# Convolution stage: token records in groups of 128, a fixed index table for the scatters, and a store of the sums of its own

## What is computed

```
x = x + conv3x3(quantize(layernorm(x)), quantized w)      # "the sums", called x3
t = tokens(x)                                             # 50176 tokens of 128 channels
h = layernorm(t) @ W_gat                                  # 16 features of a token
a_src, a_dst = (h * att_src).sum(-1), (h * att_dst).sum(-1)   # 4 heads each
# per edge: e = leaky_relu(a_src[src] + a_dst[dst]); softmax over the edges of dst; weighted sum of h[src]
```

## Time and profile before

| | us |
|---|---|
| median of 3 runs | 10784.39 |
| the runs | 10778.33 to 10784.59 |
| the profiled execution, its time | 10787.32 |
| its span, first to last instruction | 10785.5 |
| first scatter of `convolve` starts | 4175.63 |
| last scatter of `convolve` ends | 4801.45 |

### The profile page before, as it was taken

One profiled execution on the slowest core, in us unless ns is written; L12 is line 12 of the kernel. 1 busy time (PEld: TensorE's weight loads), 2 busy tenths in 40 slices (PEclk: granted clock), 3 DMA queues, 4 the chain that ended last, 5 costly groups with the idle time before them and its releaser, 6 DMA issues. The chain is left out here.

```text
span 10785.5 us, 111540 instructions
## 1 busy us (share of the span) xinstructions
PE 4563.0 (42%) x31813; PEld 2715.7 (25%) x31813; DVE 5474.9 (51%) x14162; ACT 3929.5 (36%) x9657; POOL 6184.6 (57%) x6259
## 2 busy tenths in 40 slices
PE   0011777777758997873222222223223223223000
PEld 0011555555544444541111111111111101101000
DVE  9987999999986775541121121121121112112487
ACT  0011888888854554332121111112112112112255
POOL 0000555555532224667777777777777777777675
PEclk9755999999978998876666666666666666666555
DMA  0000111111121223543222222222222222222366
GB/s 20 2 0 34 40 39 38 39 41 38 39 78 55 62 62 100 141 121 55 44 46 49 44 46 49 44 42 53 44 42 53 44 42 53 44 42 48 134 250 244
DMA packets 1326096, 663.81 MB, mean 62 GB/s; under 512 B 1058255, under 2 KB 1239100, under 8 KB 1320764
## 3 DMA queue, kind: packets, MB, share of 16 engines
q1 hardware_dynamic: 1142396, 576.49, 19.5%
q0 software_dynamic: 183104, 80.22, 5.7%
HBM read 344.86 MB, written 313.71 MB: 61 GB/s over the span
## 5 line engine op out<-in xcount | busy, mean ns | idle before, releaser
L1832 POOL DMA_INDIRECT gr_rec<-rec,gr_idx x4096 | 3954.2, 965 | 1248.8 <-issue 1248.0
L1853 PE MATMUL gr_p_h<-gr_tT,gr_w 128*128 128x512 f32 x1568 | 849.4, 696 | 3671.7 <-ACT gr_hT L1887 3638.7
L1972 DVE TENSOR_SCALAR gr_pen<-gr_same 128x64 f32<-128x64 f32 x64 | 13.7, 213 | 3170.6 <-DMA gr_rec<-rec,gr_idx 3170.6
L1853 PEld LDWEIGHTS gr_p_h<-gr_tT,gr_w 128*128 128x128 f32 x1568 | 347.6, 227 | 4154.9 <-ACT gr_hT L1887 3723.8
L544 POOL TENSOR_TENSOR at_sq<-at_qk 128x256 f32<-128x256 f32 x392 | 290.2, 740 | 1844.1 <-ACT at_qk L594 1843.9
L1900 ACT ACTIVATE gr_ee<-gr_dd 128x512 f32<-128x512 f32 x64 | 40.3, 629 | 3588.0 <-DVE gr_dd L1991 3588.0
L1858 PE MATMUL gr_p_y<-gr_hT,gr_w 128*128 128x512 f32 x1568 | 688.9, 592 | 0.0
L1952 DVE STREAM_TRANSPOSE gr_z<-gr_yb 128x2048 f32<-128x2048 f32 x98 | 226.5, 2311 | 902.8 <-issue 491.5
L1887 ACT ACTIVATE gr_hT<-gr_p_h,gr_b 128x512 f32<-128x512 f32 x784 | 517.6, 688 | 191.7 <-PE gr_p_h L1853 191.0
L2140 POOL DMA_INDIRECT cb_a<-scan,cb_idx x392 | 499.0, 1273 | 133.7 <-issue 122.4
L1340 POOL DMA_INDIRECT adst<-co_rec,co_idx x448 | 424.5, 948 | 223.3 <-issue 123.1
(11 more groups left out here) (358 smaller groups left out, 13212.1 us busy)
## 6 DMA issues: line engine op xcount, KB each, us to landing
y<-gr_z SPq DMA_DIRECT2D x392, 256.0 KB, 5.4
cb_y<-y SPq DMA_DIRECT2D x28, 3584.0 KB, 13.2
gr_rec<-rec,gr_idx POOLq DMA_INDIRECT x4096, 2.3
scan<-gr_out SPq DMA_DIRECT2D x64, 768.0 KB, 3.8
at_xs<-in_x_win SPq DMA_DIRECT2D x56, 448.0 KB, 3.8
x<-at_x SPq DMA_DIRECT2D x56, 448.0 KB, 4.2
ff_x<-x SPq DMA_DIRECT2D x56, 448.0 KB, 3.4
x<-ff_x SPq DMA_DIRECT2D x784, 32.0 KB
```

Of the source, the lines that this page charges most:

```text
L1832: nc.gpsimd.indirect_dma_start(out=rec[s][:, j, :], out_offset=None, in_=rec_dram, in_offset=bass.IndirectOffsetOnAxis(ap=idx[s][:, j:j + ...
L1853: nc.tensor.matmul(p_h[m % 4][:, :], w1[:, P * m:P * (m + 1)], tT[b.k][:, :], start=True, stop=True).then_inc(S["hp"], 1)
```

## The change

The 896 tokens of a strip are handled as seven groups of 128 instead of eight rows of 112. The record tile becomes [128 partitions, 7 groups, 24]; PE multiplies seven blocks of 128 tokens; POOL issues seven scatters. The index table is loaded as [98, 4, 128] and turned into `first` [128, 392], one column for each group of the whole image, and a scatter reads its column of this table directly: the tile `idx`, DVE's copy into it, its semaphore and DVE's wait for the scatters are gone. The rolled order shifts by 4 rows of 112 tokens, which is three and a half groups, so that the two `rec` stores become four: two of three whole groups and two of half a group. The store of the sums is issued on its own, ahead of the wait for the records, and counts on its own semaphore `x_out`, which is what DVE waits for now; tT, `recs` and the four `rec` stores count on `out`.

```
+GROUPS = WIN * W // P
+FPARTS = 4
+FROWS = B * H * W // P // FPARTS
...
-        rec = two("rec", [W, ROWS, REC])
+        rec = two("rec", [P, GROUPS, REC])
...
-        first = sb("first", [W, B * H], I32)
-        idx = two("idx", [W, ROWS], I32)
+        first = sb("first", [P, FPARTS * FROWS], I32)
...
# SP
+                        p.wait("x3", -1, 2)
+                        sp.sem_inc(S["passed"], 1)
+                        dst = x3_dram.rearrange("(y x) c -> x y c", x=W)[:, bass.ds((p.t - 1) * ROWS, ROWS), :]
+                        sp.dma_start(dst, x3[s][:, :, :]).then_inc(S[f"x_out{s}"], 16)
                         p.wait("rec", -1)
                         p.wait("tT", -1, 2)
...
-                        for dram, tile in ((x3_dram, x3), (recs_dram, rec)):
-                            dst = dram.rearrange("(y x) c -> x y c", x=W)[:, bass.ds((p.t - 1) * ROWS, ROWS), :]
-                            sp.dma_start(dst, tile[s][:, :, :]).then_inc(S[f"out{s}"], 16)
-                        for h in range(2):
-                            dst = rec_dram.rearrange("(y x) c -> x y c", x=W)[:, bass.ds(token_row(nc, p.t - 1, h), HROWS), :]
-                            sp.dma_start(dst, rec[s][:, HROWS * h:HROWS * h + HROWS, :]).then_inc(S[f"out{s}"], 16)
+                        dst = recs_dram.rearrange("(g p) c -> p g c", p=P)[:, bass.ds((p.t - 1) * GROUPS, GROUPS), :]
+                        sp.dma_start(dst, rec[s][:, :, :]).then_inc(S[f"out{s}"], 16)
+                        full = GROUPS // 2
+                        top, low = (token_row(nc, p.t - 1, h) * W for h in range(2))
+                        for row, q in ((top, 0), (low + P // 2, full + 1)):
+                            dst = rec_dram[row:row + full * P, :].rearrange("(g p) c -> p g c", p=P)
+                            sp.dma_start(dst, rec[s][:, q:q + full, :]).then_inc(S[f"out{s}"], 16)
+                        for row, lo in ((top + full * P, 0), (low, P // 2)):
+                            sp.dma_start(rec_dram[row:row + P // 2, :], rec[s][lo:lo + P // 2, full, :]).then_inc(S[f"out{s}"], 16)
# PE
-                        for r in range(ROWS):
-                            mm = nc.tensor.matmul(p_r[:, r, :], tT[s][:, r, :], wcat[:, :], start=True, stop=True)
+                        tokens = tT[s][:, :, :].rearrange("p r x -> p (r x)")
+                        for q in range(GROUPS):
+                            mm = nc.tensor.matmul(p_r[:, q, :], tokens[:, P * q:P * q + P], wcat[:, :], start=True, stop=True)
# POOL
-                        p.wait("idx", -1)
-                        pool.sem_inc(S["passed"], 1)
                         p.wait("rec", -1)
...
-                        for r in range(ROWS):
-                            nc.gpsimd.indirect_dma_start(out=adst_dram, out_offset=bass.IndirectOffsetOnAxis(ap=idx[s][:, r:r + 1], axis=0),
-                                                         in_=rec[s][:, r, FEAT + GH:REC], in_offset=None, bounds_check=E - 1,
+                        for q in range(GROUPS):
+                            g = (p.t - 1) * GROUPS + q
+                            nc.gpsimd.indirect_dma_start(out=adst_dram, out_offset=bass.IndirectOffsetOnAxis(ap=first[:, g:g + 1], axis=0),
+                                                         in_=rec[s][:, q, FEAT + GH:REC], in_offset=None, bounds_check=E - 1,
# ACT
-                        p.wait_lot("sc", -3, ROWS * 16)
+                        p.wait_lot("sc", -3, GROUPS * 16)
# DVE
-                        p.wait_lot("out", -2, CONV_OUT)
+                        p.wait_lot("x_out", -2, 16)
...
-                        p.wait_lot("sc", -2, ROWS * 16)
-                        nc.vector.tensor_copy(idx[s][:, :], first[:, bass.ds(p.t * ROWS, ROWS)]).then_inc(S["idx"], 1)
...
-CONV_OUT = 5 * 16
+CONV_OUT = 6 * 16
```

More of the change, by code:

```diff
@@ L1228, in convolve @@
         tT = two("tT", [P, ROWS, W])
-        rec = two("rec", [W, ROWS, REC])
+        rec = two("rec", [P, GROUPS, REC])
         p_c = [ps(f"p_c{i}", [P, HROWS, W]) for i in range(2)]
         p_t = [ps(f"p_t{i}", [P, HROWS, W]) for i in range(2)]
-        p_r = ps("p_r", [W, ROWS, REC])
-        first_i = sb("first_i", [H, B, W], I32)
-        first_f = sb("first_f", [H, B, W])
-        first = sb("first", [W, B * H], I32)
-        idx = two("idx", [W, ROWS], I32)
-        p_f = ps("p_f", [W, B, H])
+        p_r = ps("p_r", [P, GROUPS, REC])
+        first_i = sb("first_i", [FROWS, FPARTS, P], I32)
+        first_f = sb("first_f", [FROWS, FPARTS, P])
+        first = sb("first", [P, FPARTS * FROWS], I32)
+        p_f = ps("p_f", [P, FPARTS, FROWS])
         p_x = [ps(f"p_x{i}", [W, HROWS, P]) for i in range(2)]
@@ L1240, in convolve @@
         own = {n: ctx.enter_context(nc.semaphore("co_" + n)) for n in (
-            "consts_in", "tanh", "ext", "top", "wq", "x_in0", "x_in1", "out0", "out1", "win", "conv", "xc", "px", "x3", "stat",
-            "rstd", "t", "trp", "tT", "recp", "rec", "first", "firstp", "idx", "passed")}
+            "consts_in", "tanh", "ext", "top", "wq", "x_in0", "x_in1", "x_out0", "x_out1", "out0", "out1", "win", "conv", "xc", "px", "x3", "stat",
+            "rstd", "t", "trp", "tT", "recp", "rec", "first", "firstp", "passed")}
         S = {**own, **dict(zip(("sc0", "sc1"), d["soft"][13:15]))}
@@ L1249, in _ @@
                                  (gat[:, 0, :], d["g_wgat"]), (att[:, :, :], d["g_att"]),
[L1250 removed]
+                                 (first_i[:, :, :], start_dram.rearrange("p i -> (p i)").rearrange("(a g p) -> g a p", a=FPARTS, p=P))):
                     sp.dma_start(dst, src).then_inc(S["consts_in"], 16)
@@ L1277, in _ @@
                     sp.wait_ge(S[f"out{s}"], CONV_OUT * (STRIPS // 2))
+                    sp.wait_ge(S[f"x_out{s}"], 16 * (STRIPS // 2))
             @block.tensor
@@ L1282, in _ @@
                 pe.wait_ge(S["first"], 1)
-                for b in range(B):
-                    mm = nc.tensor.transpose(p_f[:, b, :], first_f[:, b, :], ident[0:H, 0:H])
+                for b in range(FPARTS):
+                    mm = nc.tensor.transpose(p_f[:, b, :], first_f[:, b, :], ident[0:FROWS, 0:FROWS])
                 mm.then_inc(S["firstp"], 1)
@@ L1345, in _ @@
                 for s in range(2):
-                    pool.wait_ge(S[f"sc{s}"], ROWS * 16 * (STRIPS // 2))
+                    pool.wait_ge(S[f"sc{s}"], GROUPS * 16 * (STRIPS // 2))
             @block.scalar
@@ L1391, in _ @@
                 v.wait_ge(S["firstp"], 1)
-                nc.vector.tensor_copy(first[:, :], p_f[:, :, :].rearrange("x b y -> x (b y)")).then_inc(S["first"], 1)
+                nc.vector.tensor_copy(first[:, :], p_f[:, :, :].rearrange("p a g -> p (a g)")).then_inc(S["first"], 1)
                 for k in range(2):
```

## The result

The changed kernel takes 10669.54 us (median of four runs, 10663.14 to 10682.25), the kernel before on the same chip 10781.72 us (four runs, 10778.33 to 10784.59). The ratio is 0.9898, with a 95% interval from 0.9880 to 0.9915: faster by 112 us, or 1.0%. The forecast was 10655, with a range of 10643 to 10715. The profiled execution took 10682.25 us (span 10680.5), the longest of the four.

A forecast was written before the change was run, and what follows sets the result against it. POOL's stream of scatters was taken as the bound: 392 x 0.948 + 391 x 0.305 = 490.9 us, plus 6, gave 497. 625.8 - 497 = 129 us off gave 10658 from the profiled execution, 10655 from the median; range 10643 to 10715.

The forecast's parts named there:

- One scatter of eight goes, at 0.948 each: POOL's scatters: 56 fewer at 0.948 plus a 0.305 gap each, 70.2 us off, if 128 rows cost no more than 112.
- The allowance of 6 us: POOL's stretch of scatters: 0.1 us a strip added for low-clock strips and the first strips, 6 us.
- the 4.4 us in hand: ACT's rec: ready 4.3 us after the scatters of two strips before, needed by POOL after 8.77, so 4.4 us spare.
- the main case: The graph stage's strips: POOL runs back to back at 8.75 to 9.15 us a strip, 10647 to 10672 us; 62%.
- every loop is below POOL's: Strip loops at full clock: DVE 7.3 us, ACT's branch 7.5, PE 7.2, rec to rec about 6.5, against POOL's 8.77.
- The stall's cause: Strip boundaries: late-landing scatters hold DVE's idx copy, 9.2 us from landing to POOL's restart; DVE's `rec` store wait, 94.9 us.
- at nothing left: DVE's store wait, 94.9 us: the sums' store, issued about a strip and a half before need, leaves no wait.
- ACT's wait for the scatters, 2 to 4 us a strip, harmless: ACT's rec: its wait for the scatters of two strips before stays, 2 to 4 us a strip, without delaying POOL.
- Rival 2: Scatter landing: grows from 4 to 10 us and replaces the removed wait; 9.55 us a strip, 91 won, 10693; 6%.
- Rival 4: PE: stays at 1.2 GHz, 13 us a round, 728 us for the stage, slower at 10886; 4%.
- rival 1: POOL: goes on waiting, by PE's falling clock or another wait; only the eighth scatter is won, 70 us, 10714; 22%.
- Rival 3: DVE's normalization: blocks the scatters in full, 10.91 us a strip, 611 us, 15 won, 10769, no change; 6%.

The follow-up runs named there:

- e5_six: The changed kernel with six of the seven scatters of each strip, the seventh group's a_dst not written; 10585.42 us, ratio 0.9808.
- a0_after: The changed kernel itself, nothing altered, measured once more on another chip; 10671.04 us, ratio 0.9890 to the kernel before.
- e7_rows112: The changed kernel with each of the seven scatters limited to the first 112 of its 128 rows; 10654.71 us, ratio 0.9876.
- e6_four: The changed kernel with four of the seven scatters of each strip, the other three groups' a_dst not written; 10591.04 us, ratio 0.9813.
- e1_table: The kernel before with only the fixed index table, without DVE's index copy and its wait for the scatters; 10736.76 us, ratio 0.9941.
- e3_store: The kernel before with only the store of the sums issued ahead, on its own semaphore that DVE waits for; 10748.38 us, ratio 0.9953.
- e11_table_store: The kernel before with fixed table and own store of the sums, still eight scatters of 112 rows; 10719.88 us, ratio 0.9937.
- e4_one_lot: The changed kernel with the store of the sums back among the other stores, DVE waiting for the whole lot; 10704.09 us, ratio 0.9909.
- e10_rec3: The changed kernel with three record tiles instead of two, each with its own semaphore; 10661.07 us, ratio 0.9883.

## Why the prediction was right, point by point

- **"What it shortens comes off the whole time."** Shown: the stretch gave 114.0 us, the spans 105, the medians 112. In e5_six, 80.6 us off the stretch moved the ratio from 0.9890 (a0_after) or 0.9898 (the first measurement) to 0.9808, which is 88 or 97 us, with some 25 either way by the intervals of two ratios.
- **One scatter of eight goes, at 0.948 each.** The mis-sized term. I took 0.948, the mean of scatters of 112 rows, for a scatter of 128 rows, because gathers of 128 rows cost hardly more (944); scatters measured 974, with a mean over the busy time of 0.976. 392 x (0.976 - 0.948) = 11.0 us of the miss. It was inside the bounds that the prediction gave (0.936 to 0.999), and e7_rows112 shows it to be the rows alone.
- **The allowance of 6 us.** POOL waited 0.2 us for records, so low-clock strips cost nothing, as the 4.4 us in hand should have told: then there was no term for them to add. In its place came pauses of 9.8 us, which no row of before shows. Sum of the two: 11.0 + 3.8 = 14.8 us, 511.8 against the 497 forecast. The time missed by as much, 10669.5 against 10655, and stays inside the band of the main case (10647 to 10672) by under 3 us; that the 6 us were there to take up most of the pauses is luck. Two of the signs it named did not come true: scatters of 0.94 to 0.96 us, and a last one at about 4672 (4690).
- **"DVE's wait for the scatters goes" and "every loop is below POOL's".** Shown: no wait of DVE on a DMA; 7.44 us in most strips of e6_four, 7.69 on average, against 7.5 worked out and 8.95 for POOL. (The other loop, from one rec to the next, adds up to 6.3 and not to "about 6.5", which changes nothing.)
- **The stall's cause.** Right in the main: the prediction called DVE's wait for the scatters the reason for POOL's waits, and taking it away alone (e1_table) left 0.1 of 65.1 us. Its "other stall", DVE's wait for the `rec` store, is none of its own: all 23 of these waits lie in strips that go on to wait for the scatters, and in e1_table it grew to 162.9 us at no cost. What the prediction did not have is that the own store alone takes 49 of the 65 us, with the wait for the scatters left in place (e3_store): they land sooner behind POOL's last scatter, and the way back to POOL is shorter.
- **DVE's wait for the store costed "at nothing left".** Shown, no such wait is left. What the own store is worth beside the table: nothing with eight scatters a strip (e11_table_store, 1.7 us), 21 us once the strip is 8.95 (e4_one_lot).
- **ACT's wait for the scatters, 2 to 4 us a strip, harmless.** 3.6 us a strip; e10_rec3 and e11_table_store show it harmless. The landing of 3.96 held: rec starts 3.87 after the last scatter, at a DMA share of 0.65 (0.71 was forecast). Rival 2, which needed 8.4, falls.
- **The clock, 0.9 or more.** 0.92. Rival 4 falls, and rival 1 too: POOL's waits for records went to nearly nothing.
- **The normalization beside the scatters.** DVE's normalization runs from 4402.55 to 4404.69; the two scatters beside it are

```profile
4403.19 1.06 POOL L1350 DMA_INDIRECT adst<-co_rec,co_first  x1 [0.30 <-issue]
4404.56 0.98 POOL L1350 DMA_INDIRECT adst<-co_rec,co_first  x1 [0.30 <-issue]
4405.84 0.97 POOL L1350 DMA_INDIRECT adst<-co_rec,co_first  x1 [0.30 <-issue]
```

  against 0.97 for the next: 0.1 us in this strip, not 2.14. Over the stage, the scatters that overlap a normalization have a mean of 0.978 and the others 0.970. Rival 3 falls. The rule of the Trainium skill, page "SBUF — State Buffer", section "Who interferes with whom", that VectorE in its two-port mode "fully blocks" GpSimd, does not show in this kernel; by it, as the prediction worked it out, the stretch would have been 611 us, and it is 512. Whether the normalization ran in that mode no row shows.

## What to carry over

Work out a stage as a set of loops, each with its period, and take as its length that of the longest; a wait in a loop with time in hand costs nothing, even where it grows (201 us here, 163 in e1_table). Totals of waits don't say whether two waits of an engine fall into the same strip or into different ones: look in the timeline. Where several parts of a change free the same engine, they don't add up (161 us alone, 114 together): price them in an order, the last against what the others have already won. For the cost of a DMA whose form the trace does not show, a row of the same direction with fewer rows is no nearer than one of the same rows in the other direction; keep both as bounds and lean to the dearer.

## What the runs showed of the hardware

- A scatter of 16 bytes a row costs GpSimd 942 ns with 112 rows and 974 ns with 128, while a gather of 128 rows has 947. The gap from one to the next is 0.305 us in all of them.
- GpSimd paused for 1.7 to 5.4 us at fixed counts of scatters, in some kernels and not in others whose scatters are the same, as told above.
- SP's small stores got cheaper to issue: the median of the `rec` stores was 1282 ns with two a strip, and is 672 and 580 ns now, with four; that of `recs` went from 789 to 423. Of the first kind, the rows before, now, and in e3_store:

```profile
L1274 SPq DMA_DIRECT2D rec<-co_rec x112: 513/1282/1966, 4176.4 to 4792.6; - x112
```

```profile
L1281 SPq DMA_DIRECT2D rec<-co_rec x112: 495/672/915, 4179.3 to 4678.1; - x112
```

```profile
L1278 SPq DMA_DIRECT2D rec<-co_rec x112: 327/760/890, 4177.3 to 4744.1; - x112
```

  It is the own store of the sums that does this, and not the new layout: e3_store, with two `rec` stores in the old layout, has 760 (and 421 for `recs`), while e4_one_lot, with the new layout and one lot, has 1311 (and 794). The prediction's "half-microsecond" for each of the two added issues was about right, and the old ones gave back more than that.
